# Expert stages of a graph-attention and mixture-of-experts kernel: gelu kept as two half-precision parts, three products of 128 moving columns in the output matmuls, the copies made on two engines, the shared bias folded into the experts' rows

## The reference

```python
shared = gelu(x @ W1s + b1s) @ W2s + b2s            # 128 -> 512 -> 128, every token
rw = softmax(x @ Wr);  topw, topi = top_k(rw, 2)    # 8 experts, 2 for each token
topw = topw / sum(topw)
h = gelu(x @ W1p[e] + b1p[e])                       # the same shape, for each expert e
priv[e] = h @ W2p[e] + b2p[e]
out = x + shared + sum over the two experts of topw * priv
```

## Time and profile before

| | us |
|---|---|
| median of three runs | 1407.18 (1406.4 to 1407.19) |
| the profiled execution | 1409.58 |
| its span | 1407.8 |
| TensorE busy | 1201.8 (85%) |
| GpSimd busy | 918.8 (65%) |
| VectorE busy | 729.2 (52%) |
| ScalarE busy | 686.5 (49%) |
| granted clock of TensorE, mean | 0.952 |

### The profile page before, as it was taken

The page is one execution under the profiler, slowest core; times in us unless marked ns, Lnnn a source line. Parts: engine busy times, 40 slices in busy tenths (PEclk is TensorE's granted clock), DMA queues, the critical chain, the costliest instruction groups (busy, mean ns, idle before and its releaser), DMA issues. The chain is left out here.

```text
span 1407.8 us, 34624 instructions
## 1 busy us (share of the span) xinstructions
PE 1201.8 (85%) x10884; PEld 896.5 (64%) x10885; DVE 729.2 (52%) x1894; ACT 686.5 (49%) x1158; POOL 918.8 (65%) x1009
## 2 busy tenths in 40 slices
PE   2899999999999999981899998999999999998400
PEld 1566666666666666651577777678777777887300
DVE  2689888888889889884233321010111111111198
ACT  0577676767766676760443442434443444443100
POOL 4356888888888888854667665466666666665300
PEclk9999999999999999995899999999999999999755
DMA  2013332333332332224255442544434434333399
GB/s 80 16 39 80 86 84 79 90 90 90 88 89 71 84 87 75 60 62 124 74 128 169 129 122 65 93 90 90 85 82 88 88 81 89 70 62 61 105 330 303
DMA packets 268084, 136.49 MB, mean 97 GB/s; under 512 B 170310, under 2 KB 246252, under 8 KB 268026
## 3 DMA queue, kind: packets, MB, share of 16 engines
q1 hardware_dynamic: 234490, 93.55, 27.3%
q0 software_dynamic: 16896, 33.86, 7.8%
q10 hardware_dynamic: 16640, 8.39, 2.0%
HBM read 47.95 MB, written 54.04 MB: 72 GB/s over the span
## 5 line engine op out<-in xcount | busy, mean ns | idle before, releaser
L997 PEld LDWEIGHTS Y<-w,hid 128*128 128x128 f32 x3200 | 372.6, 192 | 24.3 <-issue 11.9
L997 PE MATMUL Y<-w,hid 128*128 (+1 forms) x3200 | 376.8, 275 | 7.0 <-ACT hid L1008 5.6
L1326 POOL DMA_INDIRECT pairs_dram<-x_rows x272 | 266.0, 978 | 100.6 <-issue 100.0
L1008 ACT ACTIVATE hid<-Z,x_rows 128x512 f32<-128x512 f32 (+1 forms) x320 | 184.1, 623 | 261.6 <-PE Z L986 252.5
L1371 DVE TENSOR_TENSOR x_rows<-Y,b_rows 128x512 f32<-128x512 f32 (+1 forms) x80 | 48.9, 611 | 393.7 <-PE Y L997 359.1
L986 PE MATMUL Z<-x_rows,w 128*128 128x512 f16 (+1 forms) x960 | 191.5, 349 | 8.5 <-issue 7.4
L1104 POOL DMA_INDIRECT slots_dram<-x_rows,pair_slot x140 | 137.9, 985 | 57.6 <-issue 29.0
L475 DVE TENSOR_REDUCE smax<-S 128x8 f32<-128x1024 f32 x128 | 155.4, 1214 | 30.6 <-PE S L720 26.5
L478 DVE TENSOR_TENSOR probs<-S,smax 128x1024 f32<-128x1024 f32 x128 | 156.8, 1225 | 14.4
L617 ACT ACTIVATE probs<-probs 128x1024 f32<-128x1024 f32 x128 | 135.3, 1057 | 38.3 <-DVE probs L478 38.0
L986 PEld LDWEIGHTS Z<-x_rows,w 128*128 x960 | 92.6, 98 | 82.6 <-issue 12.0
(11 more groups left out here) (193 smaller groups left out, 1718.8 us busy)
## 6 DMA issues: line engine op xcount, KB each, us to landing
y_pairs<-pairs_dram SPq DMA_DIRECT2D x32, 512.0 KB, 6.1
x_res<-in_x_dram SPq DMA_DIRECT2D x32, 256.0 KB, 3.4
adj<-in_adj_dram SPq DMA_DIRECT2D x32, 256.0 KB, 3.0
xT_dram<-xT SPq DMA_DIRECT2D x32, 256.0 KB, 3.1
xTu<-xT_dram SPq DMA_DIRECT2D x32, 256.0 KB, 3.0
out_dram<-x_res ACTq DMA_DIRECT2D x16, 512.0 KB, 8.3
x_rows<-x SPq DMA_DIRECT2D x30, 256.0 KB, 2.7
pairs_dram<-x_rows POOLq DMA_INDIRECT x272
```

Source lines behind the costliest of these rows:

```text
L997: mm = pe.matmul(self.Y[:, b, j], self.hid[:, b, c, j * P:(j + 1) * P], self.w2[:, :, c][:, e, :], start=c == 0, stop=c == FC - 1)
L1008: act.activation(self.hid[:, b, c, 0:w], self.Z[:, c, 0:w], ACT.Gelu, bias=bias[:, c:c + 1], scale=1.0 / (XS * WS)).then_inc(self.gelu_don ...
L1326: pool.indirect_dma_start(pairs_dram, bass.IndirectOffsetOnAxis(ap=pair_of[n][:, j:j + 1], axis=0), y_sb[n % NY][:, j], None, bounds_check ...
```

## The change

Only the expert stages and the places of the first writes change.

- The gelu is kept as two half-precision parts, `h16`: a high part, the gelu by 16 rounded to half precision, and a low part, what is left. `hid` is now one float32 buffer that lies between the gelu and the parts.
- `w2` is kept as two half-precision parts too, by 64. The output matmuls make three half-precision products where one float32 matmul stood: 48 matmuls with 128 moving columns in a whole unit, 24 in a half unit.
- The high parts are made by ScalarE for the first three banks in the shared stage and the first two in the routed stage (`scaled_by_act`), by VectorE for the others. VectorE makes all low parts (`lows`).
- The readers of Y multiply by 1/(16·64) in the instruction that adds.
- The shared bias is no longer added to `x_res` in each unit. It is added once to the eight experts' bias rows, which is the same since a token's two weights sum to one. Those rows lie where the router's logits were and are loaded at the start of the shared stage.
- SyncE stages the second weights of the experts as the first ones, so VectorE splits 16 weights instead of 8. The router splits `W1s` and `W2s`.
- `SENT` goes from 27 to 29 and `KEPT` from 29 to 32: of the first writes attention makes 116, the router 12 and the shared stage none. The 8 more in attention stand behind its last loop.

```diff
-SENT = NG - 5
-KEPT = SENT + 2
+SENT = NG - 3
+KEPT = NG
...
+        for g in range(NG - 5, SENT):
+            for j in range(GT):
+                scatter(g, j)
...
     @block.scalar
     def _(act):
-        act.wait_ge(w1s_loaded, 16)
-        act.activation(w1s, w1s, ACT.Copy, scale=WS).then_inc(w_scaled, 1)
-        act.wait_ge(w_scaled, 1)
-        act.activation(f.w1[:, 0, SHARED], w1s, ACT.Copy).then_inc(w_hi, 1)
+        for n, parts in enumerate(shared_parts):
+            st = f.hid[:, n]
+            act.wait_ge(w_loaded[n], 16)
+            act.activation(st, st, ACT.Copy, scale=WS).then_inc(w_scaled, 1)
+            act.wait_ge(w_scaled, n + 1)
+            act.activation(parts[0], st, ACT.Copy).then_inc(w_hi, 1)
...
             if g == KEPT - 1:
-                pool.wait_ge(w_hi, 1)
-                pool.tensor_tensor(f.w1[:, 1, SHARED], w1s, f.w1[:, 0, SHARED], ALU.subtract).then_inc(w_lo, 1)
+                for n, parts in enumerate(shared_parts):
+                    pool.wait_ge(w_hi, n + 1)
+                    pool.tensor_tensor(parts[1], f.hid[:, n], parts[0], ALU.subtract).then_inc(w_lo, 1)
...
     def output(self, pe, u, e, b, w=UT):
 
-        pe.wait_ge(self.gelu_done, u * FC + FC)
+        pe.wait_ge(self.lo_done, u * FC + FC)
         if not (isinstance(u, int) and u < 2):
             pe.wait_ge(self.y_read, u - 1)
         for j in range(w // P):
             for c in range(FC):
-                mm = pe.matmul(self.Y[:, b, j], self.hid[:, b, c, j * P:(j + 1) * P], self.w2[:, :, c][:, e, :],
-                               start=c == 0, stop=c == FC - 1)
+                for n, (k, m) in enumerate(((0, 0), (0, 1), (1, 0))):
+                    mm = pe.matmul(self.Y[:, b, j], self.h16[:, b, k, c, j * P:(j + 1) * P], self.w2[:, m, :, c][:, e, :],
+                                   start=c == 0 and n == 0, stop=c == FC - 1 and n == 2)
         mm.then_inc(self.y_ps, 1)
...
-        for c in range(FC):
-            act.wait_ge(self.z_ps, u * FC + c + 1)
+        def hi(c):
+            act.wait_ge(self.gelu_done, u * FC + c + 1)
             if c == 0 and not (isinstance(u, int) and u < 2):
                 act.wait_ge(self.y_ps, u - 1)
-            act.activation(self.hid[:, b, c, 0:w], self.Z[:, c, 0:w], ACT.Gelu, bias=bias[:, c:c + 1],
+            act.activation(self.h16[:, b, 0, c, 0:w], self.hid[:, c, 0:w], ACT.Copy, scale=HS).then_inc(self.hi_done, 1)
+
+        for c in range(FC):
+
+            act.wait_ge(self.z_ps, u * FC + c + 1)
+            if not (isinstance(u, int) and u == 0):
+                act.wait_ge(self.lo_done, u * FC + (c + 1 - FC))
+            if 0 < c <= self.scaled_by_act:
+                hi(c - 1)
+            act.activation(self.hid[:, c, 0:w], self.Z[:, c, 0:w], ACT.Gelu, bias=bias[:, c:c + 1],
                            scale=1.0 / (XS * WS)).then_inc(self.gelu_done, 1)
...
+    def lows(self, dve, u, b, w=UT):
+
+        for c in range(FC):
+            if c < self.scaled_by_act:
+                dve.wait_ge(self.hi_done, u * self.scaled_by_act + c + 1)
+            else:
+                dve.wait_ge(self.gelu_done, u * FC + c + 1)
+                dve.tensor_scalar(self.h16[:, b, 0, c, 0:w], self.hid[:, c, 0:w], HS, None, ALU.mult).then_inc(self.scaled, 1)
+                dve.wait_ge(self.scaled, u * (FC - self.scaled_by_act) + c - self.scaled_by_act + 1)
+            dve.scalar_tensor_tensor(out=self.h16[:, b, 1, c, 0:w], in0=self.hid[:, c, 0:w], scalar=HS,
+                                     in1=self.h16[:, b, 0, c, 0:w], op0=ALU.mult, op1=ALU.subtract).then_inc(self.lo_done, 1)
...
-        firsts = NG - KEPT
-        seconds = 0
         for u in range(NG):
-
             pool.wait_ge(f.z_ps, u * FC + 1)
...
+            for t in range(u * GT, (u + 1) * GT):
+                scatter(t, 1)
...
-            dve.wait_ge(b2_added, u + 1)
             xg = x_res[:, u * GT:(u + 1) * GT, :]
-            dve.tensor_tensor(xg, f.Y[:, b], xg, ALU.add).then_inc(f.y_read, 1)
+            dve.scalar_tensor_tensor(out=xg, in0=f.Y[:, b], scalar=1.0 / (HS * WS), in1=xg,
+                                     op0=ALU.mult, op1=ALU.add).then_inc(f.y_read, 1)
...
+        dve.wait_ge(b2_in, 16)
+        dve.tensor_tensor(f.b2, f.b2, f.b2s[:].unsqueeze(1).to_broadcast([P, E, P]), ALU.add).then_inc(b2_added, 1)
         split = 0
         for u in range(U):
-            add_bias(u)
+            f.lows(dve, u, u % 2)
...
         def unit(u, n, w, w1):
+            f.lows(dve, u, n % 2, w)
             if not early(u, 1):
                 keep_y(u - 1, (n - 1) % NIN, w1)
```

More of the change, by code:

```diff
@@ L836, in router_phase @@
     block = ctx.enter_context(nc.Block())
+    shared_parts = [[f.w1[:, k, SHARED] for k in range(2)],
+                    [f.w2[:, k, SHARED].rearrange("p c d -> p (c d)") for k in range(2)]]
     @block.sync
     def _(sp):
-        sp.dma_start(w1s, d["W1s"]).then_inc(w1s_loaded, 16)
-        sp.dma_start(f.w2[:, SHARED], d["W2s"].rearrange("(c p) d -> p c d", p=P)).then_inc(w2s_loaded, 16)
+        sp.dma_start(f.hid[:, 0], d["W1s"]).then_inc(w_loaded[0], 16)
+        sp.dma_start(f.hid[:, 1].rearrange("p (c d) -> p c d", c=FC),
+                     d["W2s"].rearrange("(c p) d -> p c d", p=P)).then_inc(w_loaded[1], 16)
         sp.dma_start(f.ident[:], d["ident"]).then_inc(c_loaded, 16)
@@ L1002, in activate @@
     def activate(self, act, u, bias, b, w=UT):
+        def hi(c):
+            act.wait_ge(self.gelu_done, u * FC + c + 1)
+            if c == 0 and not (isinstance(u, int) and u < 2):
+                act.wait_ge(self.y_ps, u - 1)
+            act.activation(self.h16[:, b, 0, c, 0:w], self.hid[:, c, 0:w], ACT.Copy, scale=HS).then_inc(self.hi_done, 1)
         for c in range(FC):
             act.wait_ge(self.z_ps, u * FC + c + 1)
-            if c == 0 and not (isinstance(u, int) and u < 2):
-                act.wait_ge(self.y_ps, u - 1)
@@ L1018, in sem @@
         return ctx.enter_context(nc.semaphore(name))
+    NW = TOP * E
     NS = 4
@@ L1044, in shared_phase, with w_parts @@
     w_hi, w_split = sem("ws_hi"), sem("ws_split")
-    w2_loaded = sem("w2_loaded")
     blank_ready, tails_known, blanked = sem("blank_ready"), sem("tails_known"), sem("blanked")
     tables = sem("tables")
-    b2_added = sem("b2_added")
-    last_ids = sem("last_ids")
+    b2_added, b2_in = sem("b2_added"), sem("b2_in")
     block = ctx.enter_context(nc.Block())
     U = NG
+    w_src = [d["W1p"][e] for e in range(E)] + [d["W2p"][e].rearrange("(c p) d -> p c d", p=P) for e in range(E)]
+    def w_parts(n):
+        return [f.w1[:, k, n] if n < E else f.w2[:, k, n - E].rearrange("p c d -> p (c d)") for k in range(2)]
     def rows_gone(eng):
@@ L1065, in stage_weight @@
                 sp.wait_ge(w_split, n - NS + 1)
-            sp.dma_start(stage[:, n % NS], d["W1p"][n]).then_inc(w_staged[n % NS], 16)
+            st = stage[:, n % NS]
+            sp.dma_start(st if n < E else st.rearrange("p (c d) -> p c d", c=FC), w_src[n]).then_inc(w_staged[n % NS], 16)
         def blank_rows(at):
@@ L1249, in _ @@
                 table_of_units()
-            if u > STAGE and split < E:
+            if u > STAGE and split < NW:
                 split_weight(split)
```

69 lines of the change are left out of this document (28 added, 41 removed).

## The result

The changed kernel takes 1370.16 us (median of four runs, 1368.8 to 1371.52) where the kernel before takes 1406.79 (1406.33 to 1407.19): ratio 0.974, 95% interval 0.9723 to 0.9757. Its profiled execution took 1368.8. Forecast were 1356.4 us, 50 us of gain; 36.6 came.

The account below looks back on a forecast made before the run. TensorE was taken to pace whole units at 6.16 us, with GpSimd next. Terms -24.3 - 37.0 + 6.5 + 0.5 + 1.5 + 2 = -50.8 from 1409.6 gave 1358.8, less 2.4 for the median: 1356.4 us; 8-in-10 range 1336 to 1388.

Parts of the forecast that it names:

- half units that lengthen as a sign of being wrong: Listed as showing the prediction wrong, beside 48 matmuls over 3 us or units 6 us apart.
- TensorE's 0.056 us: Output matmuls: each half-precision matmul of 128 columns takes 0.056 us, its load hidden, so 48 take 2.69.
- The rival of load and matmul in turn: Whole units: load and matmul run one after the other, 0.080 us each, 6.43 a unit; 1441 us; chance 3%.
- Shared units, 5.40 forecast: Shared stage: each unit falls from 6.16 to 5.40 us, GpSimd's pace; over 32 units -24.3 us.
- The first rival: Whole units: GpSimd is hardly held up and TensorE paces at 5.28 us; 1340 us; chance 14%.
- The end of the shared stage: GpSimd, which had finished early, is now last there, with a landing of 1.5 us: +1.5 us.
- Whole units, 5.50 forecast: Routed stage: each whole unit falls from 6.16 to 5.50 us, GpSimd's pace; over 56 units -37.0 us.
- the upper of the two estimates: Routed whole units, DMAs meeting VectorE's operations at random: 0.4 us more per unit, given as 5.65 us.
- Attention and router, +7.0: GpSimd's four more writes and one subtraction in the router, +6.5 us; eight writes at attention's end, +0.5.
- Half units, +2 forecast: Routed half units: SyncE's 4.0 us a unit stay; low parts in the last chain add 2 us.
- "0 from TensorE": Routed half units: TensorE's saving changes nothing, as SyncE's 4.0 us stay while TensorE's work falls to 2.7.
- The rule of the exclusive port: Expert stages: VectorE and GpSimd shut each other out for whole instructions; +112 us, 1520 us; chance 4%.

Follow-up runs that it names:

- the table in pieces: The changed kernel with VectorE's small steps of table work in the shared stage spread over several units: 1365.83 us, ratio 0.9703.
- the run with that edit alone: The kernel before with only the new places of the first rows' scatters, second layer still in full precision: 1415.8 us, ratio 1.0063.
- four buffers: The changed kernel with four output buffers for the routed stage's sends in place of two: 1359.94 us, ratio 0.966.
- The fixed address: The changed kernel with four output buffers, and the half units' second product reading expert 0's weights: 1360.15 us, ratio 0.9655.
- the run of two products with the scatters unpaced: The changed kernel without the third product, with four output buffers, table work spread over units and shared-stage scatters not waiting for hidden products: ratio 1.0654.
- a job of the first kind: A job in which the kernel before took its usual time, 1406.8 to 1407.9 us, not 1513.4 or 1516.3.

## Why the prediction was right, and where its sizes were off

The time is 13.8 us above the forecast, within its range. The difference, term by term: shared +4.0, whole units -1.5, half units +7.8, combination -0.4, and +3.8 because the median of the new kernel lies 1.4 above its profiled execution while 2.4 below was carried over from the kernel before. That the two expert stages come so near is in part luck, since errors cancel: the shared term has 4.2 us too many in its units and 0.6 too many at its end, and lacks the 8.8 of the two long units. The prediction also named half units that lengthen as a sign of being wrong, and they did, by 9.8.

- **TensorE's 0.056 us**, from four matmuls of the router, held for the 48 of every whole unit: 2.68 us. The rival of load and matmul in turn fell, and with it the Trainium skill's figure.
- **Shared units, 5.40 forecast, 5.27 measured.** GpSimd was held up, its mean scatter is 1034 ns against 985, but in this stage it settled into the same phase of each unit and four scatters went by in 5.27. The first rival, in which TensorE paces, was right here.
- **The end of the shared stage** was forecast as GpSimd's (+1.5). It wasn't: VectorE's table work made TensorE the last. This is the term that I left out. In the kernel before the same steps stood in front of nothing that TensorE needed; the change put `lows` behind them, on the same engine. I asked what stands behind the new waits, and not behind the old work. It cost 8.8 us of long units, 4.6 of which GpSimd would have taken anyway, as the table in pieces shows.
- **Whole units, 5.50 forecast, 5.44 measured.** GpSimd's sends lengthened by VectorE's operations were forecast, spread over all units. Instead TensorE paced the first half at 5.27, as in the first rival. GpSimd's lag began with the stop of 2.18 us at the 114th send, which no term held, and `keep_y` waited for sends from the next unit but one on. So the size came out by a mechanism that was forecast only in part. Without `keep_y`'s wait for landings it is 5.33. (By its own terms, 5.2 + 0.4, the upper of the two estimates was 5.6 and not 5.65.)
- **Attention and router, +7.0**, measured +7.0, and +7.3 in the run with that edit alone.
- **Half units, +2 forecast, +9.8 measured.** Two pieces failed. The first half units inherit GpSimd's lag: four buffers take 4.1 us off. And "0 from TensorE" counted its matmuls alone: with eight addresses in place of four to compute for an output, its queue needs 3.97 us, as long as SyncE's 4.0, so it never makes up its lag and the last units come late. The fixed address takes 3.4 off, though with the addresses it also takes one reading of the expert's number. That is 7.5 of the 7.8.
- **The rule of the exclusive port** ("SBUF — State Buffer", "SBUF: two separate sides" in the Trainium skill) would have given 1520. The traces still agree in half. A DMA of GpSimd that begins 0.1 to 0.4 us into a low part waits for its end: in the changed kernel's trace there are 35 at low parts of 512 columns, none takes under 1.17 us, and all but the one at 718.39 end 0.83 to 0.88 after the low part. The 67 that begin in the last 0.2 us of one take 0.95 to 1.02. Readers of Y don't hold it: 71 DMAs that began under one took 0.95 to 0.99. And VectorE goes on beside the DMAs: low parts of 512 columns that begin with a DMA under way take 0.69, the others 0.71. What the rule does catch is a loop that I hadn't seen: once VectorE itself waits for GpSimd, it comes in blocks and meets every send.

## What to carry to other kernels

Where work is added to an engine, list what already stands in its queue, and ask who waits for the new work when that comes first: here 7 us of small serial steps had nothing urgent behind them until the low parts were queued there. Before making the pacing engine faster, price the next engine's floor together with the waits that tie it back; here a third fewer output matmuls made the kernel slower, and two more buffers, which TensorE never touches, gave 10 us. An engine without time to spare keeps every stop: the same 2 us cost the kernel before nothing. Count the queue's address computations beside the matmuls where units are short.

## What the hardware showed

An indirect DMA of GpSimd, 0.96 us alone, took 2.74 (the one at 718.39) while VectorE ran three low parts and a high part back to back, from 718.08 to 720.30; it got no turn between them and ended 0.83 after the last, as after a single low part.

TensorE can stand idle with nothing in the profile that it waits for. In the job where the kernel before took 1513 us, in the run of two products with the scatters unpaced, the shared stage took 315 us, 122 of them in one unit, from 738.9 to 861.4. A piece of that unit, TensorE and GpSimd:

```profile
745.81 0.58 PE L998 MATMUL Z<-xTu,w 128*128 128x512 f16 x1 [2.21 <-issue]
745.99 0.96 POOL L1144 DMA_INDIRECT slots_dram<-x_rows,pair_slot  x1 [0.31 <-issue]
...
747.92 0.59 PE L998 MATMUL Z<-xTu,w 128*128 128x512 f16 x1 [1.52 <-issue]
748.52 0.96 POOL L1144 DMA_INDIRECT slots_dram<-x_rows,pair_slot  x1 [0.30 <-issue]
```

GpSimd sends a scatter every 1.26 us, and TensorE gets one matmul every 2.1 to 2.8 with nothing in the profile that it waits for. The unit ends with the scatters, the last of which begins at 860.19; the next unit takes 20.3, and then they are 4.4 to 5.7 apart. In the runs of these jobs whose scatters are paced by the hidden products the shared stage took 211 to 223 us. So the pace that looks idle may protect the others; this was seen only in these jobs, in one run that had three more edits, and an unpaced run in a job of the first kind wasn't made.
